# Attention and feed-forward on one core: the start-up of the first chunk reordered, with q of chunk 0 in two halves

## The reference

```python
def xattn(KEY, VALUE, QUERY, ...):           # KEY = VALUE = ctx, QUERY = layernorm(x)
    k, q, v = heads(KEY @ Wk.T + bk), heads(QUERY @ Wq.T + bq), heads(VALUE @ Wv.T + bv)
    score = einsum('bhij,bhkj->bhik', k, q) / sqrt(dh)
    attn = softmax(score, axis=1)             # over the 16 heads
    out = einsum('bhik,bhij->bhjk', attn, v)
    return reshape(out) @ Wo.T + bo

def qlora_linear(x, q, scale, bias, la, lb):
    w = (q / 7.5 - 1.0) * repeat(scale, 16, axis=1)
    return x @ w.T + bias + (x @ la.T) @ lb.T

x = x + xattn(ctx, ctx, layernorm(x), ...)
h = layernorm(x)
for blk in range(3):
    y = gelu(layernorm(qlora_linear(h, 2 * blk), gamma, beta))
    h = qlora_linear(y, 2 * blk + 1) + h
x = x + h
```

## Time and profile before

| | us |
|---|---|
| median of three runs | 377.6 |
| lowest and highest | 377.5, 378.43 |
| profiled execution, its own time | 380.3 |
| its span in the profile | 378.5 |
| TensorE products busy | 340.5 (90%) |
| VectorE busy | 330.5 (87%) |
| ScalarE busy | 289.5 (76%) |
| GpSimd busy | 267.6 (71%) |

### The profile page before, as it was taken

How to read it: one execution, slowest core, us unless ns; L and a number is a source line. 1 busy time by engine, 2 the same in 40 slices (tenths; PEclk the granted TensorE clock), 3 DMA queues, 4 the chain that set the end, 5 groups by cost and what they waited for, 6 DMA issues and landing times.

```text
span 378.5 us, 12988 instructions
## 1 busy us (share of the span) xinstructions
PE 340.5 (90%) x4772; PEld 253.0 (67%) x4772; DVE 330.5 (87%) x826; ACT 289.5 (76%) x577; POOL 267.6 (71%) x264
## 2 busy tenths in 40 slices
PE   3766899999999999999979786889999999999984
PEld 2343556776677667766756564776788888888863
DVE  6437999999999999999998999869999999988752
ACT  7646887888788878887866554557989999999862
POOL 6321988788788877887887878967778778774321
PEclk9979999999999999999998999899999999999999
DMA  5593764685467546854651400000001001100112
GB/s 156 152 286 111 216 212 141 192 248 168 142 190 237 176 138 197 237 168 145 202 196 53 145 2 2 3 2 0 3 29 58 28 28 38 48 29 29 55 43 71
DMA packets 53122, 43.29 MB, mean 114 GB/s; under 512 B 4496, under 2 KB 46944, under 8 KB 53088
## 3 DMA queue, kind: packets, MB, share of 16 engines
q1 hardware_dynamic: 53088, 42.84, 37.7%
HBM read 26.05 MB, written 16.78 MB: 113 GB/s over the span
## 4 chain that ended last, share of the span: by engine, by line
PE 60%; DVE 21%; issue 8%; ACT 4%; POOL 3%; DMA 2%; SPq 1%; POOLq 0%; DVEq 0%; ACTq 0%
PE score_ps L1240 9%; PE att_ps L1216 7%; PE score_ps L1159 6%; PE wo_ps L1031 5%; DVE zsum L694 5%; DVE negmax L680 5%; PE score_ps L1043 3%; PE work L1067 3%; DVE st L717 3%; PE work L1301 3%; PE score_ps L1308 3%; PE score_ps L1234 2%; PE att_ps L1308 2%; PE work L1073 2%; PE work L1080 2%
## 5 line engine op out<-in xcount | busy, mean ns | idle before, releaser
L444 POOL TENSOR_TENSOR probs<-probs,rz 128x1024 f32<-128x1024 f32 x64 | 136.2, 2140 | 40.7 <-DVE rz L697 40.5
L455 POOL TENSOR_TENSOR rs<-ve,minus_half 128x4 f32<-128x4 f32 (+1 forms) x50 | 59.4, 1187 | 43.1 <-DVE ve L633 31.7
L882 ACT ACTIVATE probs<-score_ps 128x1024 f32<-128x1024 f32 x64 | 65.6, 1025 | 26.0 <-PE score_ps L1159 25.6
L680 DVE TENSOR_REDUCE negmax<-score_ps 128x64 bf16<-128x1024 f32 x64 | 75.2, 1175 | 4.8 <-PE score_ps L1043 4.7
L694 DVE TENSOR_REDUCE zsum<-probs 128x64 f32<-128x1024 f32 x64 | 77.3, 1208 | 1.6 <-ACT probs L882 1.6
L930 ACT ACTIVATE z<-score_ps,rs 128x128 f32<-128x128 f32 x160 | 46.0, 384 | 2.8 <-POOL rs L455 2.8
L1159 PE MATMUL score_ps<-negmax,ident_bf 128*128 128x512 bf16 x128 | 39.2, 388 | 9.7 <-DVE negmax L680 9.6
L1240 PEld LDWEIGHTS score_ps<-lin_t,h 128*128 128x128 f32 x320 | 39.0, 192 | 12.6 <-DVE h L755 7.7
L1031 PEld LDWEIGHTS wo_ps<-wo_t,att_t 128*128 128x128 f32 x256 | 37.3, 193 | 13.7 <-issue 12.1
L1240 PE MATMUL score_ps<-lin_t,h 128*128 128x128 f32 x320 | 42.3, 280 | 3.3 <-ACT probs L882 1.1
L1216 PE MATMUL att_ps<-probs,v_diag 128*32 128x64 f32 x2048 | 43.4, 225 | 1.6 <-POOL probs L444 1.4
(11 more groups left out here) (184 smaller groups left out, 672.2 us busy)
## 6 DMA issues: line engine op xcount, KB each, us to landing
q_parts<-parts SPq DMA_DIRECT2D x16, 512.0 KB, 3.5
k_stack<-k_parts SPq DMA_DIRECT2D x32, 256.0 KB, 3.4
q_stack<-q_parts SPq DMA_DIRECT2D x64, 128.0 KB, 2.9
ctx_sb<-in_ctx SPq DMA_DIRECT2D x16, 256.0 KB, 3.7
k_parts<-parts SPq DMA_DIRECT2D x16, 256.0 KB, 2.9
out<-x_all SPq DMA_DIRECT2D x16, 256.0 KB, 2.3
x_all<-in_x SPq DMA_DIRECT2D x14, 256.0 KB, 3.8
x_all<-in_x SPq DMA_DIRECT2D x1, 512.0 KB, 4.9
```

Source lines behind the costliest of these rows:

```text
L444: nc.gpsimd.tensor_tensor(e[:, :, :, :], e[:, :, :, :], by_query.broadcast_to([P, BANDS, SEQ, ADJ]), ALU.mult).then_inc(s_probs, 1)
L455: nc.gpsimd.tensor_tensor(rs2[v][:, lo:hi], ve2[v][:, lo:hi], minus_half[:, lo:hi], ALU.pow).then_inc(p_rs[v], 1)
L680: nc.vector.tensor_reduce(negmax[p % 2][:, :], score_ps[p % 2][:, :].rearrange("p (h k) -> p k h", k=SEQ), AX_X, ALU.max, negate=True).the ...
L882: nc.scalar.activation(probs[p][:, :, :, :], score_ps[p % 2][:, :].rearrange("p (u s k) -> p u k s", s=ADJ, k=SEQ), ACT.Exp, scale=SCALE). ...
```

## The change

The prologue is reordered, and three things move out of it into chunk 0.

- q of chunk 0 is made in two halves of 256 tokens (`first_input`, `first_transposes`, `first_q`, `first_q_remainder`, `first_q_part`): the first half in wo_ps, the second in work0. Each half and part is stored on its own (four stores of a quarter of q), and gathered half by half (eight transfers); scores(0, 0) waits for the first half alone, pair 2 for the second. k of chunk 0 is turned into its parts on VectorE (`first_key_parts`) in place of ScalarE and gathered by two transfers that ScalarE issues behind the normalised input of chunk 1.
- `scores(0, 0)` comes right after k and q of chunk 1, ahead of `project_v(0)`, the low-rank products and the layers. `value_blocks(0)` goes behind the first exponential on ScalarE; the low-rank products go to chunk 0, pair 0; effective_weights on VectorE goes behind the first negmax; the layers go to pair 1; first_layer_rows and first_layer_seeds go from pair 0 to pair 2.
- The low-rank factors are laid out anew: lora_b is turned in six pieces to 32 partitions, and the six products stand in the same 32 rows of the array (before, four strips of rows were used). The additions of w_eff are two wide ones in place of six, the copies to lin_t two in place of six.
- Loads: the loads of the bias rows are issued by ScalarE; ctx of chunk 0 goes ahead of wq; the load of chunks 2 and 3 of x goes ahead of the stores of q and k.
- Eight products of the identity with itself (`keep_awake`), whose result nobody reads, stand at TensorE's start.
- The variance of chunks 1 and 2 goes from GpSimd to VectorE. The clearing of v_diag goes from ScalarE to GpSimd, in pieces of 512 columns, as does that of q_stack[1], now behind the power of chunk 1. The pick_row copies and the two casts of the identity go ahead of the first statistics on VectorE.

```diff
@@ gpsimd
+            def clear(tensor, done):
+                for i in range(4):
+                    ins = nc.gpsimd.memset(tensor[:, 512 * i:512 * (i + 1)], 0.0)
+                ins.then_inc(done, 1)
...
             def prologue():
-                pool.wait_ge(s_veps, 1)
-                input_scale()
-                nc.gpsimd.memset(q_stack[1][:, :, :, :].bitcast(F32), 0.0).then_inc(s_const, 1)
-                nc.gpsimd.memset(one_col[:, :], 1.0).then_inc(s_const, 1)
+                first_scale(0)
                 pool.wait_ge(s_const, 2)
                 nc.gpsimd.tensor_scalar(centre[:, :], ident[:, :], -1.0 / D, None, ALU.add).then_inc(s_const, 1)
-                input_variance(1)
-                input_variance(2)
+                nc.gpsimd.memset(one_col[:, :], 1.0).then_inc(s_const, 1)
+                first_scale(1)
+                clear(q_stack[1][:, :, :, :].bitcast(F32).rearrange("p g s t -> p (g s t)"), s_const)
+                clear(v_diag[0], s_vzero)
+                first_scale(2)
+                clear(v_diag[1], s_vzero)
@@ vector
             def prologue():
                 pick_columns()
-                dve.wait_ge(s_xin[0], 16)
-                input_stats_of(0)
-                first_variance()
+                identities()
+                next_input(0)
                 centred_query_weights()
-                identities()
                 bias_columns()
+                first_key_parts()
+                next_input(1)
+                output_weights()
                 bias_parts()
-                dve.wait_ge(s_xin[1], 16)
-                dve.wait_ge(s_rstd, 1)
-                input_stats_of(1)
-                output_weights()
-                feed_forward_weights()
+                low_rank_rows()
+                dequantised_weights()
+                next_input(2)
...
                     if isinstance(c, int) and c == 0 and p == 0:
+                        effective_weights()
+                    if isinstance(c, int) and c == 0 and p == 2:
                         first_layer_seeds()
@@ scalar
+            def gather_first_k():
+                act.wait_ge(s_k_out, 16)
+                src = k_dram[0].rearrange("(g r) l t -> (r l) g t", g=GROUPS)
+                for a in range(2):
+                    act.dma_start(k_stack[0][a:P:2, :, :], src).then_inc(h_k_stack, 16)
...
                 if live(c):
                     exponentials(0)
+                if isinstance(c, int) and c == 0:
+                    act.wait_ge(s_v_ps, 1)
+                    act.wait_ge(s_vzero, 2)
+                    value_blocks(0, 0)
...
                 if live(c + 2):
                     q_high(c + 2, par)
                     q_low(c + 2, par)
+                if isinstance(c, int) and c == 0:
+                    transposed_layers()
@@ tensor
+            def keep_awake(count):
+                for i in range(count):
+                    nc.tensor.matmul(bank[6][:, 0:P], ident[:, :], ident[:, :], start=True, stop=True)
...
                 k_remainder(1, 1)
                 q_remainder(1, 1)
+                pe.wait_ge(h_k_stack, 16 * 2)
+                pe.wait_ge(h_stack, 16 * SLOTS)
+                pe.wait_ge(s_lbt, 1)
+                scores(0, 0)
                 pe.wait_ge(s_pick, 2 + len(BIAS_ROWS))
                 pe.wait_ge(s_split, 7)
                 pe.wait_ge(s_q_lo, 2)
+                pe.wait_ge(s_wready, 5)
                 project_v(0)
-                for u in range(NLIN // 2):
-                    transpose_layers(u)
-                pe.wait_ge(s_stack[0], 16 * STACK_DMAS)
-                scores(0, 0)
...
-                    if isinstance(c, int) and c == 0 and p == 0:
-                        first_layer_rows()
+                    if isinstance(c, int) and c == 0:
+                        if p == 0:
+                            low_rank_products()
+                        elif p == 1:
+                            transpose_layers()
+                        elif p == 2:
+                            first_layer_rows()
```

More of the change, by code:

```diff
@@ L110, in build @@
         w_eff = sb("w_eff", [P, NLIN, P])
-        lb_t = [sb("lb_t0", [P, P]), sb("lb_t1", [2 * RANK, P])]
+        lb_t = sb("lb_t", [RANK, NLIN, P])
         lin_t = sb("lin_t", [P, NLIN, P])
@@ L803, in q_high @@
                 act.wait_ge(s_q_ps, k + 1)
-                if some(k - 1):
-                    act.wait_ge(s_q_out, 16 * (k - 1))
+                if isinstance(k, int) and k == 2:
+                    for u in range(2):
+                        act.wait_ge(h_q_out[u], 16 * 2)
+                elif some(k - 2):
+                    act.wait_ge(s_q_out, 16 * (k - 2))
                 nc.scalar.activation(parts[par][:, 0, 0, :], work0[:, :], ACT.Identity,
@@ L850, in prologue, with first_input, first_columns, first_q_part @@
                 nc.scalar.activation(cols_h[:, :], bank[3][:, NROWS:2 * NROWS], ACT.Copy).then_inc(s_wready, 1)
-                input_columns(0)
-                act.wait_ge(s_wready, 4)
-                k_high(0, 0)
-                q_high(0, 0)
-                k_low(0, 0)
-                q_low(0, 0)
+            def first_input(u, done):
+                for t in (2 * u, 2 * u + 1):
+                    ins = nc.scalar.activation(xln[:, t, :], x_all[:, 0, t, :], ACT.Copy, scale=half_rstd[:, t:t + 1])
+                ins.then_inc(done, 1)
+            def first_columns(u, src, ready, done):
+                act.wait_ge(ready, 1)
+                nc.scalar.activation(xln_t[:, half_columns(u)], src[:, half_columns(u)], ACT.Copy).then_inc(done, 1)
+            def first_q_part(u, l, src, ready, done):
+                act.wait_ge(ready, 1)
+                nc.scalar.activation(parts[0][:, 0, l, half_columns(u)], src[:, half_columns(u)], ACT.Identity,
+                                     bias=cols_h[:, ROW_BQ:ROW_BQ + 1]).then_inc(done, 1)
+            def gather_first_k():
[3 more added lines that the diff above has]
+                    act.dma_start(k_stack[0][a:P:2, :, :], src).then_inc(h_k_stack, 16)
+            def prologue():
+                bias_loads()
+                transposed("k", bank[1], 1)
+                act.wait_ge(s_rstd, 1)
+                first_input(0, h_xln)
+                context_columns(0, 0)
+                transposed("q", bank[0], 2)
+                first_columns(0, wo_ps, h_xln_ps, h_xln_t)
+                bias_columns()
+                first_input(1, s_xln)
+                act.wait_ge(s_wready, 4)
+                first_q_part(0, 0, wo_ps, h_q_ps, h_q_hi)
+                first_q_part(0, 1, wo_ps, h_q_rest, h_q_lo)
+                first_columns(1, work0, s_xln_ps, s_xln_t)
+                first_q_part(1, 0, work0, s_q_ps, s_q_hi)
+                first_q_part(1, 1, work0, s_q_rest, s_q_lo)
+                normalised_input(1)
+                gather_first_k()
+                context_columns(1, 1)
+                input_columns(1)
+                k_high(1, 1)
+                q_high(1, 1)
+                k_low(1, 1)
+                q_low(1, 1)
                 transposed("v", bank[2], 4)
```

249 lines of the change are left out of this document (142 added, 107 removed).

## The result

| | before | changed kernel |
|---|---|---|
| median of 20 runs each, same chip | 378.35 us | 376.93 us |
| lowest and highest | 375.29 to 380.31 | 373.36 to 379.21 |
| profiled execution, its own time | 380.3 | 373.36 |
| its span | 378.5 | 371.6 |

The ratio is 0.995, interval 0.9927 to 0.9974. The changed kernel is faster, by some 1.9 us (1.0 to 2.8) by the ratio and by 1.4 between the medians. The forecast was 374.0, a gain of 3.6. The median lies in the range given, but in its upper end, beyond the times of rival 1 and within those of rival 3, and half of the forecast gain or more isn't there. The kernel before is also 0.75 us slower over 20 runs than the three runs had shown.

The account below looks back on a forecast made before the run. VectorE, full in the attention chunks, bounds the kernel, so its first unbroken run must start earlier. Scores 8 us earlier leave 4.0 at pair 4, less 0.4 for memsets: 377.6 - 3.6 = 374.0 us, range 371.5 to 377.2.

Parts of the forecast that it names:

- rival 1: Prologue: project_k still at 1.2 GHz (1.3 us) or gathers 1 to 2.5 us later; 375.3 to 376.5 us; chance 0.23.
- rival 3: Late prologue plus slow clock for project_v and low-rank products leave no gain: 377.6 us, give or take 1; chance 0.13.
- the two places named: Chunk 0, VectorE: waits for low-rank products before negmax(1), 5.9 us gained; for the seeds' rows before negmax(3), 4.0 gained.
- The 30.8 for pair 2: Chunk 0: forecast start of negmax(2), from negmax(1) at 26.9 and the old distance of 3.6.
- The copies of pick_row: Front, VectorE: held by GpSimd's memset to 3.3, then 1.0 us with the casts; statistics 0.5 us late (bounds 0 and 0.6).
- The stores and gathers of q: Prologue stacks: stores taken at the earlier 3.6 us, gathers landing about 4 us after issue; first q landed by 20.6.
- The 0.4 us taken off for the memsets: Prologue, 14 to 19 us: VectorE's bias_parts and w_deq meet memsets in four pieces; 0.4 us lost (bounds 0 and 1.5).
- Nothing of the change is left: Behind negmax(4): VectorE is full from there, so the 4.0 us gained go unchanged to the end.
- the median of the runs is 377.6, 2.7 lower for the same work: Whole run: profiled 380.3 us set against a 377.6 median, from which the 3.6 us gain was subtracted.
- The prediction's own sign of being wrong: Wrong if negmax(4)'s gain isn't the run's, VectorE rests after 42 us, or first scores don't come before 24 us.
- rival 4: TensorE at 1.2 GHz from before project_v through the layers, also slow in front: 2.8 us slower, 380.4 us; chance 0.06.
- the 2.44 that I took as a measure of safety: TensorE, 8 to 25 us: no rest above some 1.5 us expected, against 2.44 before the earlier clock fall.

Follow-up runs that it names:

- a_third: The changed kernel, unedited, run a third time for one more profile; 376.78 us, ratio 0.9951 to the kernel before.
- a_fifth: The changed kernel, unedited, run once more for its trace; 376.29 us.
- a_fourth: The changed kernel, unedited, run once more for its trace; 373.86 us (two runs).
- a_again: The changed kernel, unedited, run once more; 375.72 us, ratio 0.9948 to the kernel before.
- b_awake: The kernel before with twelve dummy products in TensorE's rest ahead of the low-rank products; 377.92 us, ratio 0.9997.
- a_warm: The changed kernel with 13 more dummy products where TensorE waits in the start-up; 373.88 us, ratio 0.9894 to the kernel before.
- a_noawake: The changed kernel without its eight dummy products at the start; 376.83 us, ratio 0.9962 to the kernel before.

## Why the prediction was half right

**What held.** The way the change works, and its course through chunk 0. First scores 20.45 (20.7 forecast), negmax of pairs 0 to 4 at 20.91, 26.90, 30.52, 35.21, 38.06 (21.2, 26.9, 30.8, 35.2, 38.0), VectorE's wait for w_eff 2.92 (2.7) and for the seeds 0.56 (0.6). Four of eight us at the scores are paid back, at the two places named. (The 30.8 for pair 2 was a slip of the sum: 26.9 and the old distance of 3.6 make 30.5, which is what came.) The copies of pick_row are held by the memset, which ends at 3.28: they take 1.46 us and end at 3.84. The statistics came 0.3 late, not 0.5. rows_h, free of a memset, took 0.32 (1.64 before). That a gain at pair 4 is whole at pair 63 held too.

**Steps that were mis-sized.** project_k was put at 2.4 GHz (1.0 us) and took 1.67 us in the first profile, 2.08 in a_third and a_fifth, 1.55 in a_fourth and 1.13 in a_again: the eight dummies don't settle the clock there. The stores and gathers of q were put too long, by 1.5 and some 1 us. That the first scores met their forecast is luck in this sense, the two errors having opposite signs. The 0.4 us taken off for the memsets that VectorE meets wasn't there (the mark was hit without it, and the distance to pair 63 is the same in both kernels). "Nothing of the change is left" behind pair 4 missed the 0.6 us that the changed kernel gains from the 13th gelu step on.

**The step that failed** is the one from the profiled execution to the median: "the median of the runs is 377.6, 2.7 lower for the same work", and with it the gain of 4.0 read as that of every run. The first profile of before was of a late kind: 380.3, where its 147 runs have a median of 378.35. The 2.7 us were in part the very thing that the change was credited with removing. With all nine profiles, the mark of before is at 41.17 in the mean and that of the changed kernel at 38.65, 2.5 us apart: 0.9 of the missing 1.5 because before's first was late, 0.6 because the changed kernel's is later in two of five. Over all runs the medians are 378.35 (147) and 375.94 (54), 2.4 apart; the first 20 runs of the changed kernel, 376.93, were 1.0 above that, which no trace explains. That 2.5 and 2.4 agree proves little: the 0.6 us behind pair 63 comes on top of the 2.5. The prediction's own sign of being wrong, that the gain at pair 4 isn't what the run gains, is met in the medians.

**The rivals.** The measured 376.93 lies between the times of rivals 1 and 3 and could be read as either; the traces show neither in every run. The rivals were treated as cases for all runs, with a chance each. They are what happens in some executions. The late front (rival 1) is in a_third, 1.2 us at pair 4; the clock falling in chunk 0 (rival 4) in a_fifth, 2.7 us at pair 4, though only from the layers on, and for 1.49 us of rest ahead of it, less than the 2.44 that I took as a measure of safety. A share of such executions belonged in the forecast itself. With more of the gaps filled, neither is in the three profiles, and the median is 374.02 over 18 runs, 4.3 below before.

**What stays open.** How often each fall of the clock comes in the runs without a trace; what VectorE waited for in the 0.49 us above. The nine profiled executions differ by 4.0 us in the mean, the runs by 2.1, so they aren't a fair sample, and the shares of fast and late executions read from them are uncertain. And b_awake: its profile has the mark 1.3 us earlier than the mean of before, and its median is 0.4 lower only. Its profile had low clock at 196 to 200 and 230 to 234 us; whether filling the one gap makes these likelier wasn't tested. Nor was the kernel before with as many gaps filled as a_warm has, so how much of the 4.3 is the reordering and how much the dummies isn't known.

The later falls have places that were left as they are. Between 40 and 360 us TensorE has only two rests above 1.3 us, the same in all 17 profiles: one of 2.03 to 2.08 us that ends at 192.6 to 197.6, and one of 2.14 to 2.17 that ends at 226.9 to 233.2. Every fall recorded between 40 and 360 us begins near the end of one of them: at the first within 1.2 us, at the second within 5.5. Both rests end with a shift that waited for VectorE's negmax. Dummy products there are the next thing to try; no run has them.

## What to carry to other kernels

Where TensorE has gaps in a start-up, take several profiles of the kernel before and read the clock of each stretch before counting a slow stretch as something that a change removes; otherwise the forecast's base is one draw out of several. A reordering that fills TensorE's rest in one place may open it in another (here ahead of the shift of pair 1), and dummy products in those gaps, each behind a wait that keeps them off the path, go with times of 374.54 us or less in 15 of 18 runs, against 14 of 54 without the 13 products. And a step of VectorE that is moved must be looked at against what GpSimd runs at its new time, also at the time that it has in an execution with low clock.

## What the runs showed of the hardware

- TensorE's clock falls to 1.2 GHz (0.50) at different places from one execution of the same program to the next: at 16 to 20, 23 to 30 or 24 to 28 us before, at 8 to 12, 28 to 32 or 34 to 38 in the changed kernel, and later around 195 and 235 us in some. A fall near 195 us costs 1.2 to 1.4 us (between pairs 53 and 57 in the first profile of before, a_again and a_third), although VectorE is full there otherwise: it then waits 0.8 us in all for ScalarE's exponentials.
- It fell behind a rest of 1.49 us in a_fifth and a_noawake and didn't fall at the same place, behind the same rest, in the first profile of the changed kernel and in a_again. Near 195 us all 17 profiles have the same rest of TensorE, 2.03 to 2.08 us; in 8 of them the clock fell within 1.2 us of its end, in 9 it didn't.
- The record can show full clock where the durations are those of 1.2 GHz: in a_third the stretch from 8 to 10 us has 1.00, and project_k took 2.08 us in it. The same holds for the kernel before, where it took 1.91 at a recorded 1.00. So a low clock in the first 10 us can be missing from the column in the table above.

```profile
8.00:10.00 2.00, 2.00 (x5) 1.12 (x5) 0.00 (x0) 1.28 (x6) 0.00 (x0) 1.00 1.21 221
...
8.46 2.08 PE L1167 MATMUL work<-ctx_tr,w_t_k 128*128 128x512 f32 x2
```

- A VectorE instruction on two columns can cost a microsecond when it meets a long GpSimd multiply (seed_mean, 1.08 for 0.17). By the Trainium skill, page SBUF — State Buffer, section Who interferes with whom, a `tensor_scalar` such as this can take the port pair that VectorE shares with GpSimd; whichever engine issued first then holds the pair for its whole instruction, and the other waits. The trace agrees: the multiply was under way (from 35.22), and seed_mean ended 0.03 us behind it.
